# The first attention steps after the modulation: a written-out order for every engine in place of loops with hooks

## What is computed

```python
x = _L0(x, theta, phi)           # rotate channels in groups of four
# L1, the modulation: two layer norms over a whole sample, two 512x512 products
out = silu(scale * _layer_norm(x, gamma, beta) + shift) @ W_in + b_in
x = silu(scale * _layer_norm(out, gamma, beta) + shift) @ W_out + b_out + x
# L2, the steering: a basis from two Gram-Schmidt runs of 32 columns, and a gate
U_o, V_o = gram_schmidt(U), gram_schmidt(V)
basis = U_o @ V_o.T
x = x + strength * (((x @ basis) @ basis.T[:, :R]) @ resp_w.T + resp_b + safety_bias)
# L3: attention with 16 heads of 32, causal, then a feed-forward of 2048 and a gate
h = layernorm(x, gamma1, beta1); Q, K, V = h @ Wq + bq, h @ Wk + bk, h @ Wv + bv
x1 = x + softmax(causal(Q K^T / sqrt(32))) V @ Wo + bo
x2 = x1 + gelu(layernorm(x1, gamma2, beta2) @ W1 + b1) @ W2 + b2
return x + g * (x2 - x)
```

## Time and profile of the kernel before

| | |
|---|---|
| median of three runs | 1706.26 us |
| lowest, highest run | 1700.8, 1706.82 us |
| the profiled execution, its own time | 1705.07 us |
| its span in the trace | 1703.3 us |
| mean granted clock of TensorE over the span | 0.976 of full |
| PE, DVE, ACT, POOL busy | 1633.5, 1162.8, 989.0, 403.7 us |
| start of blocks 10, 11 and 13 on PE | 167.21, 179.14, 203.61 us |
| first score of steps 0, 1, 2, 3, 4 | 281.63, 299.84, 321.18, 342.54, 366.96 us |

### The profile page before, as it was taken

The page is one execution under the profiler, slowest core; times in us unless marked ns, Lnnn a source line. Parts: engine busy times, 40 slices in busy tenths (PEclk is TensorE's granted clock), DMA queues, the critical chain, the costliest instruction groups (busy, mean ns, idle before and its releaser), DMA issues.

```text
span 1703.3 us, 27189 instructions
## 1 busy us (share of the span) xinstructions
PE 1633.5 (96%) x9318; PEld 1316.6 (77%) x9318; DVE 1162.8 (68%) x2767; ACT 989.0 (58%) x2329; POOL 403.7 (24%) x606
## 2 busy tenths in 40 slices
PE   6799998899999999999999799999999999999999
PEld 4588766667777777777776478878999999999998
DVE  7799865768787878777766448767565656565643
ACT  5688843777777777787877545534242424242432
POOL 5788620222222222222221102020202020101010
PEclk9899998989999999999999799999999999999999
DMA  7122233434444444444344515666746464646451
GB/s 306 60 82 82 86 124 77 129 71 129 99 127 100 126 100 125 103 122 110 95 97 112 198 51 204 247 223 246 257 158 252 161 248 169 247 173 248 173 198 68
DMA packets 61825, 254.78 MB, mean 150 GB/s; under 512 B 10581, under 2 KB 15957, under 8 KB 45945
## 3 DMA queue, kind: packets, MB, share of 16 engines
q1 hardware_dynamic: 61688, 253.06, 45.5%
HBM read 153.93 MB, written 48.23 MB: 119 GB/s over the span
## 4 chain that ended last, share of the span: by engine, by line
PE 85%; DVE 6%; DMA 3%; ACT 2%; issue 1%; SPq 1%; POOL 1%; DVEq 0%; POOLq 0%; ACTq 0%
PE psum L83 22%; PE psum L84 21%; PE psum L85 21%; PE psum L1928 5%; PE psum L1909 5%; PE psum L1956 5%; DMA k_raw<-in_w_in 1%; PE psum L1852 1%; DVE psum L1191 1%; PE psum L1860 1%; PE psum L3082 1%; DMA k_raw<-d 1%; PE psum L1842 0%; PE psum L1827 0%; DMA out<-k_result 0%
## 5 line engine op out<-in xcount | busy, mean ns | idle before, releaser
L1191 DVE CUSTOM_DVE_ANT_0 psum<-psum,b_mask 128x512 f32<-128x512 f32 (+3 forms) x512 | 242.9, 509 | 92.1 <-PE psum L1909 87.6
L1534 ACT ACTIVATE psum<-psum,b_mx 128x512 f32<-128x512 f32 (+3 forms) x512 | 258.0, 506 | 74.3 <-DVE b_mx L1191 71.9
L2991 ACT ACTIVATE k_act<-k_stack_f,k_smalls 128x512 f32<-128x512 f32 x112 | 81.0, 723 | 338.1 <-DVE k_stack_f L2779 338.1
L1544 ACT ACTIVATE k_exps<-psum 128x512 f32<-128x512 f32 (+1 forms) x384 | 196.4, 528 | 84.7 <-PE psum L1928 83.6
L1058 POOL TENSOR_SCALAR_AFFINE_SELECT k_exps<-k_exps 128x256 f32<-128x256 f32 x256 | 96.1, 412 | 458.8 <-ACT k_exps L1544 458.8
L2632 POOL TENSOR_SCALAR k_result<-k_result,k_pb 128x512 f32<-128x512 f32 x32 | 59.9, 1889 | 454.2 <-DVE k_result L2698 454.2
L2758 DVE TENSOR_TENSOR k_act_lo<-k_act,k_act_hi 128x512 fp32r<-128x512 f32 x112 | 77.3, 690 | 130.1 <-ACT k_act_hi L2994 130.1
L1928 PE MATMUL psum<-k_stack 98*128 98x512 f32 (+3 forms) x512 | 141.7, 340 | 12.6 <-ACT k_exps L1544 7.1
L83 PE MATMUL psum<-k_act_hi,k_w_hi 128*128 128x512 f32 x384 | 150.9, 393 | 0.6 <-DVE k_act_lo L2758 0.6
L84 PE MATMUL psum<-k_act_lo,k_w_hi 128*128 128x512 f32 x384 | 150.6, 392 | 0.0
L85 PE MATMUL psum<-k_act_hi,k_w_lo 128*128 128x512 f32 x384 | 150.3, 391 | 0.0
(11 more groups left out here) (377 smaller groups left out, 4445.3 us busy)
## 6 DMA issues: line engine op xcount, KB each, us to landing
k_stack<-w_factors SPq DMA_DIRECT2D x35, 1792.0 KB, 7.7
k_stack<-k_samples SPq DMA_DIRECT2D x384, 128.0 KB, 2.4
k_weights<-w_factors SPq DMA_DIRECT2D x17, 1792.0 KB, 7.7
x<-k_tokens SPq DMA_DIRECT2D x10, 1024.0 KB, 3.9
k_tokens<-x SPq DMA_DIRECT2D x8, 1024.0 KB, 5.2
d<-k_result SPq DMA_DIRECT2D x32, 256.0 KB, 2.9
k_raw<-x SPq DMA_DIRECT2D x8, 1024.0 KB, 4.9
k_raw<-d SPq DMA_DIRECT2D x8, 1024.0 KB, 7.1
```

Source lines behind the costliest of these rows:

```text
L1191: last = dve.tensor_tensor_reduce(got, got, mask[:, S - width:S], -INV_SQRT_DH, -2.0 * MASKED, ALU.add, ALU.min, mx[n % 2][:, h, t:t + 1])
L1534: act.activation(sc(n, u)[:, at:at + width], sc(n, u)[:, at:at + width], ACT.Exp, bias=mx[n % 2][:, h, t:t + 1], scale=-1.0, accum_out=sum ...
L1544: act.activation(exps[n % 2][:, h, at:at + width], by_key(n, u)[:, 0:width], ACT.Exp, scale=INV_SQRT_DH).then_inc(k_act, 1)
L2991: act.activation(act_f[:], whole_tile, ACT.Gelu, bias=small(smalls, "b1", 2 * pair % M + second)).then_inc(pair_gelu, 1)
```

## The change

The loops of the modulation stop after k = 4 (`PREFIX = 5`) and the attention's loop runs over steps 4 to 29 only (`STEADY`). For what lies between, block 10 to the end of step 3, each engine gets a function that is a plain list of calls: `sync_head`, `gpsimd_head`, `vector_head`, `scalar_head`, `tensor_head`. Five more (`..._tail`) do so for the last steps and the start of the feed-forward. The hooks `ahead(k, part)`, `beside(n, u)` and the conditions on sample numbers go away. The order of bank uses is two tables, `HEAD_USES` and `TAIL_USES`, around the rule for the steady steps, and waits that were in the loops are now in the pieces that need them (`values_out`, `attention_result`, `sample_in`, `score`). Every engine has the instructions that it had, up to a few memsets and table loads that stand in another place. The order differs on PE in rows 588 to 1150 of 7805, on DVE in rows 210 to 500, on ACT in rows 134 to 310 of 1627, on POOL in rows 188 to 235, on SP in rows 37 to 70 and at some 400. Steps 4 on have the order of before, and so has the tail, except that on SP the second half of the first feed-forward weight is loaded ahead of the second weight.

The core of the diff, with a few lines of each of the long lists:

```diff
-        for k in range(B + 1):
-            first, second = AT.get((1, k)), AT.get((0, k + 2))
+        for k in range(PREFIX):
+            first, second = AT[1, k], AT[0, k + 2]
             if k:
                 gs_columns()
-            if first is not None:
-                deviation(first)
-            gs_columns(3 if k in FOUR or not k else 2)
-            if second is not None:
-                deviation(second)
-        ahead()
+            deviation(first)
+            gs_columns(3)
+            deviation(second)
...
-            if place == B - 2:
-                if part == 3:
-                    strengths(0)
-                    coefficients()
-                if part == 5:
-                    steering(1)
-                if part == 6:
-                    steering(2)
-                if part == 4:
-                    steering(3)
-                    steering(4)
-                    steering(5)
-                    p_low(0)
-            if place == B - 1:
-                if part == 0:
-                    steered(0, 0)
-                    steered(0, 1)
-                if part == 1:
-                    steered(0, 2)
-                    steered(0, 3)
-                if part == 5:
-                    for t in range(T):
-                        statistics(0, t)
-                if part == 4:
-                    for t in range(T):
-                        normalise(0, t)
-                    weight_low(1)
-            if place == B:
-                if part == 1:
-                    split_low(0)
-                    split_low(1)
-                if part == 3:
-                    split_low(2)
-                if part == 5:
-                    split_low(3)
-                if part == 4:
-                    weight_low(2)
-                    result_constants()
...
+def gpsimd_head(mod, att):
+    att.mask_and_low()
+    mod.deviation(12)
+    mod.gs_columns(1)
+    mod.gs_columns(3)
+    mod.deviation(13)
+    mod.gs_columns(1)
+    mod.gs_columns(2)
+    mod.deviation(14)
+    mod.deviation(15)
+    att.prepare_rstd(0)
+    att.stacked_ones()
+    att.prepare_rstd(1)
...
+def vector_head(mod, att):
...
+    mod.centre(14)
+    att.coefficients()
+    mod.low(13, 0)
+    att.steering(1)
+    mod.spread(14)
+    mod.low(13, 1)
+    att.steering(2)
...
+    mod.finish(7, 3)
+    att.max_unit(0, 0)
+    att.values_out(0, 0)
+    att.strengths(1)
+    att.max_unit(0, 1)
+    att.values_out(0, 1)
+    att.max_unit(0, 2)
...
+    att.output_bias()
+    att.wo_low(0)
+    att.max_unit(0, 11)
...
+def scalar_head(mod, att):
...
+    att.weight_high(0)
+    mod.squares(12)
...
+    mod.squares(15)
+    att.weight_high(1)
+    for k in range(4):
+        att.tokens_out(0, k)
+    mod.silu_high(15, 0)
+    mod.silu_high(15, 1)
+    att.weight_high(2)
...
+def tensor_head(mod, att):
...
+    mod.half_tile(12, 3, 1)
+    att.p_first(0)
+    att.p_first(1)
+    att.steering(1)
+    att.p_first(2)
+    att.p_first(3)
+    mod.half_tile(13, 0, 0)
+    att.steering(2)
...
+    mod.half_tile(14, 1, 0)
+    att.tokens_in(0, 0)
+    att.tokens_in(0, 1)
+    mod.variance(15)
+    mod.half_tile(14, 1, 1)
+    att.tokens_in(0, 2)
+    att.tokens_in(0, 3)
...
+    mod.half_tile(15, 1, 1)
+    for k in range(8):
+        att.qk_piece(0, 0, k)
+    mod.half_tile(15, 2, 1)
+    mod.half_tile(15, 3, 1)
+    att.p_in_groups(1)
+    att.v_piece(0, 0, 0)
+    att.v_piece(0, 0, 1)
+    att.gate_first(1)
+    att.v_piece(0, 0, 2)
+    att.v_piece(0, 0, 3)
+    att.score(0, 0)
+    att.score(0, 1)
+    att.gate_second(1)
+    for k in range(4):
+        att.v_piece(0, 1, k)
+    att.score(0, 2)
...
+    att.score(0, 8)
+    att.output_bias()
+    att.steer_piece(1, 0)
...
```

More of the change, by code:

```diff
@@ L1322, in ahead, with first_sum @@
-        def ahead(place, part=None):
+        def first_sum(half):
+            if half == 0:
+                dve.wait_ge(sample_ld, 32)
+            for j in (2 * half, 2 * half + 1):
+                dve.tensor_tensor(first[:, j, :], first[:, j, :], first_d[:, j, :], ALU.add).then_inc(mid_set, 1)
+        def ahead(place):
             if place == "start":
                 gate_constants()
-            if (place, part) == (0, 1):
+            if place == "row high":
                 row_high()
-            if (place, part) == (0, 4):
+            if place == "row low":
@@ L1489, in vector, with slots @@
         groups = (first_group, second_group, third_group, fourth_group)
-        def slots(after):
-            for n in SLOTS:
-                if steady(n):
-                    groups[n % G](n, n // G)
-                    continue
-                for u in range(STEPS):
-                    if u == 4 and 0 <= n + 1 < GROUPS:
-                        qk_out(n + 1, 1)
-                    if 0 <= n < GROUPS:
-                        max_unit(n, u)
-                    beside(n, u)
-                    after(n, u)
-        return ahead, slots
+        def slots():
+            for n in STEADY:
+                groups[n % G](n, n // G)
+        return steps(ahead, strengths, coefficients, steering, p_low, steered, statistics, normalise, weight_low, split_low, result_constants,
+                     qk_out, values_out, max_unit, shift_rows, maxima_out, ctx_low, attention_result, output_bias, wo_low, first_sum, slots)
     def scalar(act):
@@ L3062, in samples @@
                     period(b, p)
-        return after, samples
+        return steps(w1_high, w2_high, factor_high, tokens, scale, block_high, gelu, samples)
     def tensor(pe):
```

2009 lines of the change are left out of this document (1320 added, 689 removed), and 6 rows, old and new, of the table HEAD_USES.

## The result

The changed kernel takes 1676.48 us (median of four runs, 1673.9 to 1677.54) beside 1705.95 us of the kernel before: a ratio of 0.983, with a 95% interval from 0.981 to 0.985. The profiled execution took 1676.03 us, with a span of 1674.2. The four medians of the kernel before that stand beside the kernels of this document are 1705.95, 1704.75, 1701.79 and 1702.95 us, so the gain is 25 to 30 us, and two medians of different groups are not to be compared to better than some 4 us. What follows goes by stretches of the traces.

The account below looks back on a forecast made before the run. PE's 19.7 us idle and 41 us at low clock, between 203.6 and 367, were taken as the bound. -13.9 + 2.5 - 1.4 - 1.3 - 3.5 = -17.6 took 1705.07 to 1687.5 us, range 1677 to 1702.

Parts of the forecast that it names:

- the ceiling of 35 us: From 203.6 to 367 us, the most that order alone could gain, from PE's idle time and low clock.
- the signs that I had named: Trace readings expected, such as first score near 267.7, last column near 210, steering wait 3 to 6 us, step 3 near 21.
- A: Blocks 11 to 13: POOL's mask and subtractions, moved ahead of the Gram-Schmidt tail, cost 7.9 us (0 to 14).
- Its first term: Block 11: PE gets a low part late because POOL's subtractions delay deviation(12); 1.6 us (0 to 3).
- A's second term: Ahead of block 13: PE stands at the first steering product, waiting for the last column; 4.7 us (0 to 9).
- 5.7 each: POOL's Gram-Schmidt columns: time taken for each of the first five, read from the trace before; last column ending at 210.3.
- Rival 1: Gram-Schmidt columns could end by 206 and not make PE wait, so no loss there: 1679.6 us; chance 0.20.
- B: Block 13 to first score: 21.8 us leave the 78.0, as waits, low-clock loss and work moved behind the score.
- C: Step 0 of the attention takes in the moved work and lengthens from 18.2 to 20.7 us: +2.5 (0 to +5.4).
- D, E, F: Steps 1, 2 and 3 of the attention shorten through the new order: -1.4, -1.3 and -3.5 us.
- The tail: Last steps: the one exchanged load has steady work over it, so it costs nothing.
- Rival 4: Steps 0 to 3 and around the steering stall: PE at low clock for 100 us, making 1717 us; chance 0.10.

Follow-up runs that it names:

- e4: Kernel before's order through block 15 and q and k of step 0, then the changed kernel's order to the end of step 3; 1683.07 us, ratio 0.988.
- e1: Changed kernel with POOL's mask and four subtractions back after deviation(15), as before the change; 1676.87 us, ratio 0.985.
- e5: Changed kernel with POOL's mask and four subtractions moved to after deviation(14), where POOL was idle; 1674.55 us, ratio 0.984.
- e7: Changed kernel with the pieces moved among step 0's scores put ahead of the first score again; 1683.63 us, ratio 0.989.
- e9: Changed kernel with step 3 in the order of before on PE, DVE and ACT; 1683.67 us, ratio 0.989.
- e10: Changed kernel with step 3 in the order of before on PE alone; 1681.41 us, ratio 0.988.
- e2: Changed kernel with the tail's two weight loads on SP in their order of before; 1671.41 us, ratio 0.982.

## Why the prediction was right or wrong

**What bounds the kernel** held: the ceiling of 35 us, made of 19.7 us idle and the time at the low level, and the windows in which it lay. From the end of block 12 to the first maximum of step 4, the part that the ceiling was for, the changed kernel won 35.7 us, all of it (163.9 to 128.2); 3.2 of that had been lost in blocks 11 and 12. Of the signs that I had named, the subtractions (171 to 178), the shift beside them (2.15), step 0 (20.5 at 0.87) and step 4 (20.2 in both) came as written. The wait of 3 to 6 us at the steering, the last column (205 for 210), the first score (19.3 earlier for 13.9) and step 3 (15.7 for 21) did not. That the subtractions end where I had them, 178.0 for 177.7, is luck: the mask ahead of them took 1.9 us on POOL and not 1 at most, and they took 7.0 and not 8.0.

**A, the step that failed first.** Expected 7.9, measured 3.2. Its first term, the late low part in block 11, was expected at 1.6, and the stretch grew by 3.2. 2.4 of it is idle time of PE in the first row above. The other 0.8 goes with the three waits: products follow each other every 0.23 us but last 0.39 in the trace, so that each idle time is counted 0.16 short, and the first product after one holds the next back by 0.1 more. The way was another one too: I had deviation(12) late behind the subtractions in POOL's queue, and it was DVE's stretched instructions that came late. A's second term, the stall of 4.7 at the steering, was not there at all, nor the 1.6 of low clock behind it. The failing step is "5.7 each" for a column. That number came from a stretch in which POOL and DVE disturb each other, and I carried it to another order. The six columns took 36.0 us before (168.90 to 204.93) and 36.0 in e4 with the old order, but 25.4 in the changed kernel and 25.4 in e1 as well, where the mask is elsewhere. POOL's idle time within them fell from 3.7 to 0.2 (now DVE waits for the columns instead, 0.4 to 1.1 us four times), two deviations of 0.56 no longer stand among them, and its own instructions took about 6 us less. PE for its part came to the steering at 209.2 and not at 207.1, and by then the result of the columns was there. Rival 1 came true in its mechanism (it had the columns end by 206), though A was not 0. That it is DVE's order which sets the columns' time is read from the timelines; no run changed it alone. That subtractions slow DVE by 0.85 to 1.0 per instruction and not by their whole length held: 3.0 us were lost beside 7.02 us of POOL. The Trainium skill (SBUF — State Buffer, Who interferes with whom) calls the shared ports of the two an exclusive lock; an estimate by that rule is a loss of up to 7. The trace shows 3 for DVE, and it shows the other side too: POOL's subtractions took 1.76 each here and 1.50 in e5, where one such instruction of DVE was beside them (1.48).

**B, right.** Expected 21.8 off the 78.0, measured 23.2 (78.8 to 55.6). The moved pieces are 7.8 (e7) where 2.8 + 4.0 + 1.1 stood; with the 1.4 for a piece of q, which no run parts off, 14.0 are left for waits and low clock, where 7.5 + 5 stood.

**C, right in size, wrong in meaning.** +2.5 expected, +2.3 measured. But e7 shows that most or all of step 0's growth is made good in steps 1 and 2.

**D, E, F, mis-sized.** -1.4, -1.3 and -3.5 expected, -5.1, -2.0 and -7.7 measured, 8.6 us more in all. This is the largest miss. I had the right bound, "17 at full clock" for step 3, and then took a value half way to before. (It came at 15.7, since some of its products now stand in step 2: 97 for 104 in the window.) The reason I gave, the waits, was worth some 7 us in these steps; what I left out of the sum is that the time at the low level went with the waits. PE's busy time in steps 1 to 3 fell from 60.0 to 52.1 us with the same 307 products. e9 has both back in one step, and e10 shows that the second need not follow from the first: there the waits are back and the clock is not down.

**The tail, wrong.** "The moved store on SP and the tail's one exchanged load have steady work over them; nothing" was +4.3 for the load. There is no steady work over it: the last maxima rows wait behind 2 MB, and PE idles for them (e2).

**The sum.** The misses are -4.7 (A), -1.4 (B), -0.2 (C), -8.6 (D to F), +4.3 (tail) and -0.9 elsewhere: -11.5, from 1687.5 to the 1676.0 of the profiled run. Rival 4, more time at the low level, went the other way: from 41 us to under 8.

## What to carry to other kernels

Where an engine waits and its clock falls with it, cost the two together: here the order that ended the waits won the low-clock time as well, and the time at full clock was a better forecast than a value half way. The sum of the waits alone does not tell what the clock does: 2.7 us of them left it at 1.00 in one kernel, 3.3 us came with 0.85 in another. A duration read in a stretch where two engines disturb each other belongs to that order; for another order take its smallest instances as one bound. Before a small transfer that the end of a stage waits for, look at what stands ahead of it in the queue: a large load put there was worth 4 us, in a change worth 29.
